# An eight-sequence, four-layer kernel: the first layer's scan moved beside the two 16-head attentions, its preparation beside the last layers

## The reference, cut to what matters

```
x = x + mamba(ln(x))            # L0: bidirectional selective scan, 256 channels, 16 states
x = x + experts16(ln(x))        # L0: 16 small experts, top 2 of the top groups
x = x + attn_relbias(ln(x))     # L1: 16 heads of 64, learned position bias
x = x + linear_with_lora(ln(x)) # L1
x = x + attn_rope(ln(x))        # L2: 16 heads of 8, rotary, causal
x = x + block(ln(x))            # L2: attention of 16 heads of 8 (rotary), norm, 8 experts
                                #     (512 wide, gelu), norm
x = x + memory(ln(x))           # L3: a recurrent outer-product memory
x = x + experts8(ln(x))         # L3: 8 experts (256 wide, gated)
```

```
xi, z = split(xn @ in_proj.T)
xc    = silu(causal_conv(xi))                     # for both directions
dt, Bm, Cm = split(xc @ xproj)
delta = softplus(dt @ dtproj + bias)
h_t   = exp(delta_t * A) * h_(t-1) + delta_t * xc_t * Bm_t   # for 16 states
y_t   = sum over states of h_t * Cm_t
out   = (0.5 * y_f + 0.5 * reversed(y_b)) * silu(z) @ out_proj.T + residual
```

## Time and profile before

| | us |
|---|---|
| median of the runs | 5811.86 |
| the profiled execution | 5812.37 |
| its span, first to last instruction | 5810.6 |
| start of sequence 0's moe0 | 225.57 |
| start of sequence 1's moe0 | 940.55 |
| start of the eighth's moe0 (z stages) | 5234.68 |

### The profile page before, as it was taken

One profiled execution on the slowest core, in us unless ns is written; L12 is line 12 of the kernel. 1 busy time (PEld: TensorE's weight loads), 2 busy tenths in 40 slices (PEclk: granted clock), 3 DMA queues, 4 the chain that ended last, 5 costly groups with the idle time before them and its releaser, 6 DMA issues. The chain is left out here.

```text
span 5810.6 us, 67170 instructions
## 1 busy us (share of the span) xinstructions
PE 4485.7 (77%) x20516; PEld 2226.2 (38%) x20516; DVE 3772.0 (65%) x8877; ACT 3064.0 (53%) x5351; POOL 1140.3 (20%) x1356
## 2 busy tenths in 40 slices
PE   5786778877788777887778777788778877788777
PEld 2342434424344243442434324343243433444334
DVE  6756586565865658656686556865668555686554
ACT  3365645556455555555655556555565555555443
POOL 2401132011320123201231012310123111231100
PEclk8996989978898788987889878897789987899778
DMA  4210021100210002100121001210012100121000
GB/s 160 87 36 1 21 65 55 32 1 25 67 55 26 1 28 71 52 22 1 34 73 47 20 1 37 75 48 13 1 42 75 46 11 1 44 73 47 7 1 2
DMA packets 104076, 218.53 MB, mean 38 GB/s; under 512 B 11072, under 2 KB 19776, under 8 KB 103152
## 3 DMA queue, kind: packets, MB, share of 16 engines
q1 hardware_dynamic: 103680, 213.81, 11.6%
HBM read 211.08 MB, written 2.69 MB: 37 GB/s over the span
## 5 line engine op out<-in xcount | busy, mean ns | idle before, releaser
L859 POOL TENSOR_TENSOR slot_work<-slot_work,slot_c_all 128x512 f32<-128x512 f32 x448 | 570.2, 1273 | 1015.9 <-DVE slot_work L942 1015.0
L777 PE MATMUL BANKS<-slot_work,WF 128*128 128x512 f32 x896 | 530.5, 679 | 5.7 <-DVE slot_du L918 2.9
L524 ACT ACTIVATE attn_prob<-BANKS 128x512 f32<-128x512 f32 (+3 forms) x896 | 401.5, 532 | 122.5 <-PE BANKS L426 119.0
L1000 PEld LDWEIGHTS BANKS<-WF,slot_x_a 128*128 128x128 f32 x2688 | 359.3, 197 | 264.5 <-ACT slot_x_a L1040 133.5
L1000 PE MATMUL BANKS<-WF,slot_x_a 128*128 128x128 f32 x2688 | 373.3, 283 | 86.3 <-ACT slot_x_a L1040 86.3
L1010 PE MATMUL BANKS<-XT,WF 128*128 128x512 f32 x768 | 425.3, 639 | 2.6 <-ACT slot_comb_t L306 2.6
L769 PE MATMUL BANKS<-slot_bcs,WB 96*128 96x512 bf16 x448 | 189.1, 422 | 305.1 <-DVE slot_work L942 304.0
L202 POOL TENSOR_TENSOR rstd<-rstd,WF 128x4 f32<-128x4 f32 x40 | 40.3, 1007 | 1572.7 <-DVE rstd L220 1559.5
L1809 DVE CUSTOM_DVE_ANT_0 attn_biased<-BANKS,attn_toep 128x512 f32<-128x512 f32 x448 | 306.0, 684 | 51.9 <-PE BANKS L1707 46.6
L1788 ACT COPY attn_probt<-BANKS 128x512 f32<-128x512 f32 x448 | 261.0, 583 | 147.3 <-PE BANKS L1714 144.4
L426 PE MATMUL BANKS<-attn_parts_kT,attn_parts_qT 64*128 64x512 bf16 (+3 forms) x896 | 309.2, 437 | 33.6 <-ACT attn_parts_qT L504 20.7
(11 more groups left out here) (674 smaller groups left out, 9464.7 us busy)
## 6 DMA issues: line engine op xcount, KB each, us to landing
slot_c_all<-c_rows SPq DMA_DIRECT2D x448, 256.0 KB, 3.1
attn_toep<-bias_line SPq DMA_DIRECT2D x112, 448.0 KB, 4.4
first_c_all<-c_rows SPq DMA_DIRECT2D x64, 256.0 KB, 3.1
WF<-in_wf SPq DMA_DIRECT2D x4, 1964.0 KB, 16.2
zattn_toep<-bias_line SPq DMA_DIRECT2D x16, 448.0 KB, 4.3
WF<-in_wf SPq DMA_DIRECT2D x3, 800.0 KB, 17.2
WF<-in_wf SPq DMA_DIRECT2D x3, 785.5 KB, 6.0
XIN<-in_x SPq DMA_DIRECT2D x8, 256.0 KB, 2.9
```

The costliest lines, as they stand in the source:

```text
L524: nc.scalar.activation(prob[:, i % PR, lo:hi], bank("T", i), ACT.Exp).then_inc(exped, 1)
L777: nc.tensor.matmul(SUM, ident, work[:, m % RW, :], start=(n == 0), stop=(n == NS - 1)).then_inc(acc, 1)
L859: nc.gpsimd.tensor_tensor(work[:, m % RW, :], work[:, m % RW, :], c_all[:, m % RC, :], ALU.mult).then_inc(rd, 1)
L1000: last = nc.tensor.matmul(DOWN[e % 2][:, j * D:(j + 1) * D], a1[:, i % 3, j * P:(j + 1) * P], w_down[:, i * D:(i + 1) * D], start=(t == 0 ...
```

## The change

The first layer becomes two functions. `mamba_pre` is its preparation and leaves its results in buffers that are kept (`M_KEPT`). `mamba_scan` is the 64 steps and the projection behind them. Its result goes to a new buffer XM, since X is still in use, and DVE copies XM to X in the last stage.

The two attentions are rewritten as streams with due times (`rope_parts`, `head8_parts`, `back_parts`; one unit is due every 1.0) and run in one block, heads, beside `mamba_scan` of the next sequence (a step is due every 3.6). `last_layers` runs in the stage last beside `mamba_pre` of the sequence after the next. Ahead of the loop there are now p0 (preparation of sequence 0), s0 (its scan, alone) and p1 (preparation of sequence 1, alone). The loop has six turns. A copy (y) does the seventh sequence: it has a scan beside its heads and no preparation. The copy z does the eighth, with neither.

The heads get four banks for everything instead of six for scores plus two for the rest, because the scan keeps three: two for its products instead of three, and one for the sum. In a step DVE now multiplies for step s and later scans the same step s. The decay ring has 4 places instead of 5, the work ring 6 instead of 8.

The weights of moe2 no longer lie in SBUF. They come by DMA, 512 KB for each expert, into a ring of three. The next input comes by DMA at the start of last, where before it came during attn1.

```diff
-    def mamba(st, after=None):
-        RD, RW, RC, AHEAD, FLUSH = 5, 8, 3, 5, 4
-        PRE, SCAN, STEP = 13.5, 52.0, 2.6
+    def mamba_pre(st, fetch):
+        PRE = 13.5
+        zs, xc, delta, du, bcs = M_KEPT
...
         def sync(sp):
+            yield -3.0
+            sp.dma_start(XIN[:, :, :], fetch()).then_inc(xin_ld, 16)
...
+    def mamba_scan(st, dest, START, STEP):
+        RD, RW, RC, LATE = 4, 6, 3, 2
+        SUM, DRIVE, OUT = PS[0], (PS[1], PS[2]), PS[1]
...
+            for s in range(STEPS):
+                d, t, n = step(s)
+                yield at(s)
+                dve.wait_ge(b_cast, s + 1)
+                V.tensor_tensor(DRIVE[s % 2], DRIVE[s % 2], du[:, d, t, :], ALU.mult).then_inc(drv, 1)
+                if s >= NS and n == LATE:
+                    yield at(s) + 0.2 * STEP
                     flush(s // NS - 1)
+                yield at(s) + 0.5 * STEP
+                dve.wait_ge(drv, s + 1)
+                dve.wait_ge(dec, s + 1)
+                if s >= RW:
+                    dve.wait_ge(acc, s - RW + 1)
+                V.tensor_tensor_scan(work[:, s % RW, :], decay[s % RD], DRIVE[s % 2], 0.0,
+                                     ALU.mult, ALU.add).then_inc(scn, 1)
...
+        def sync(sp):
+            for e in range(E if stream is not None else 0):
+                yield at - 10.0 if e < RW else at + 0.2 + step * tiles_per * (e - RW + 1)
+                if e >= RW:
+                    sp.wait_ge(used, tiles_per * (e - RW + 1))
+                sp.dma_start(ring_w[:, e % RW, :], stream[e]).then_inc(w_ld[e % RW], 16)
...
+            if copy_next:
+                dve.wait_ge(freed, 1)
+                nc.vector.tensor_copy(X[:, :, :], XM[:, :, :])
...
+    def both_attentions(st, at, u):
+        RING, WEIGH = PS[3:7], PS[7]
...
+    with Stage("p0") as st:
+        layer = mamba_pre(st, lambda: one(xs, 0))
+    with Stage("s0") as st:
+        layer = mamba_scan(st, X, 2.0, 1.95)
+    with Stage("p1", last=True) as st:
+        layer = mamba_pre(st, lambda: one(xs, 1))
...
+        with Stage("heads", last=True) as st:
+            streams = [mamba_scan(st, XM, 4.0, 3.6)] if scan_next else []
+            streams.append(both_attentions(st, 0.0, 1.0))
...
+        with Stage("last", last=True, at_end=store) as st:
+            streams = [mamba_pre(st, lambda: one(xs, b + 2))] if pre_next else []
+            streams.append(last_layers(st, scan_next))
...
+    with nc.Fori(0, n - 2) as b:
+        layers(b, True, True)
```

More of the change, by code:

```diff
@@ new lines, in back_parts, with tensor, scalar, gpsimd @@
+    def back_parts(st, tag, heads, O, turned_o, w_o, add_to, banks, at, bias=None):
+        tn, ev, dn, ch, added = (st.sem(f"{tag}_{n}") for n in ("tn", "ev", "dn", "ch", "added"))
+        def tensor(pe):
+            yield at
+            pe.wait_ge(heads.o_normed, heads.groups)
+            for j in range(NJ):
+                last = nc.tensor.transpose(banks[0][:, j * P:(j + 1) * P], O[:, j, :], ident)
+            last.then_inc(tn, 1)
+            yield at + 1.6
+            pe.wait_ge(ev, 1)
+            for j in range(NJ):
+                last = nc.tensor.matmul(banks[1][:, j * P:(j + 1) * P], turned_o[:, j * P:(j + 1) * P], w_o,
+                                        start=True, stop=True)
+            last.then_inc(dn, 1)
+        def scalar(act):
+            yield at + 0.9
+            act.wait_ge(tn, 1)
+            nc.scalar.copy(turned_o[:, :], banks[0][:, :]).then_inc(ev, 1)
+        def gpsimd(pool):
+            return
+            yield
+        def vector(dve):
+            link = Chain(dve, ch)
+            if bias is not None:
+                yield at
+                link(nc.vector.tensor_tensor(add_to[:, :, :], add_to[:, :, :], bc(bias.unsqueeze(1), [P, NJ, D]), ALU.add))
+            yield at + 2.8
+            dve.wait_ge(dn, 1)
+            nc.vector.tensor_tensor(add_to[:, :, :], add_to[:, :, :], banks[1].rearrange(tiles, j=NJ), ALU.add).then_inc(added, 1)
+        pieces = Pieces()
+        pieces.tensor, pieces.scalar, pieces.gpsimd, pieces.vector, pieces.added = tensor, scalar, gpsimd, vector, added
+        return pieces
@@ L2016, in store @@
             sp.dma_start(one(ys, b), XO[:, :, :]).then_inc(x_free, 16)
-        def clear(sp):
-            for stage in stale:
-                for s in stage.sems:
-                    sp.sem_clear(s)
-        with Stage("slot", last=True, at_end=store) as st:
-            taken = st.sem("x_taken")
-            streams = [mamba(st, after=(taken, 1))] if ahead else []
-            streams.append(last_layers(st, taken))
+        with Stage("heads", last=True) as st:
+            streams = [mamba_scan(st, XM, 4.0, 3.6)] if scan_next else []
+            streams.append(both_attentions(st, 0.0, 1.0))
```

929 lines of the change are left out of this document (481 added, 448 removed).

## The result

The changed kernel takes 5850.65 us (median of 4 runs, 5847.08 to 5863.06) against 5811.82 for the kernel before beside it: a ratio of 1.0071, 95% interval 1.0054 to 1.0089. It is slower by 0.7%, where 0.9% faster was forecast. The profiled execution has a span of 5852.3 us, 41.7 more than before.

The account below looks back on a forecast made before the run. No engine was taken as full; DVE's scan moves from slot to the attentions. Six turns of 703.2 us against 715.6 give -74, with -48, +4 and +67 elsewhere: -51, so 5760 us, range 5665 to 5885.

Parts of the forecast that it names:

- term 1: Heads with a scan, seven times: DVE's 231.9 us of work at a share of 0.843 gives 275 us.
- the share of 0.843: DVE's busy part of heads, taken from nearby rows where other layers ran beside scan steps (84% and 85%).
- Rival A: Heads set by PE and its banks, in each attention's first 25 us at clock 0.50: 290 us, 5865 total; chance 0.23.
- A's sign: Clock of 0.50 through the heads' start, and maxima or scan's multiplication waiting for PE over 40 us in a stage.
- Rival B: Heads and last together keep DVE's share of 0.68, so a turn gains nothing: 5835 us; chance 0.10.
- The argument against it: Against no gain in DVE's share: 59% alone became 84% with the scan beside; moe3 53% alone, 85% with steps.
- Rivals C and D: C: DVE at 0.91, heads 255 us, 5620 total, chance 0.15. D: last 10 us longer, 5820 total, chance 0.08.
- Terms 2 and 3: 2: last with a preparation, six times, 218.6 us. 3: seams, 6.9 us between turns, 2 between heads and last.
- Term 4: The seventh sequence (y), scan beside heads but no preparation: 667.3 us, a change of -48.
- Term 5: The eighth sequence (z), neither scan nor preparation: 187.5 us for the attentions, 2 for the seam, 2 for the rest: +4.
- Term 6: Ahead of the loop, p0, s0 and p1 in series: 238.6 us, +67, with s0 at 1.93 us a step.

Follow-up runs that it names:

- noscan: The changed kernel with no scan beside the heads in any turn (first layer's result left out): 5252.1 us.
- masked: The changed kernel with the causal maxima's masked scores written to SBUF in bf16 in place of back into their bank: 5818.4 us, ratio 1.001.
- blank: The changed kernel with the five memsets of heads due 8 later, behind GpSimd's first product: 5851.5 us, ratio 1.0088.
- port: The changed kernel with GpSimd's product with row C cut to 16 of 512 columns: 5766.2 us, ratio 0.993.
- early: The changed kernel with the matmul that spreads row B (L683) due 2.9 ahead of its multiplication in heads in place of 1.0: 5774.1 us, ratio 0.9939.
- best08: The changed kernel with L683 due 2.9 ahead, masked scores to SBUF, heads' memsets later and last's preparation due 4.5 later: 5741.7 us, ratio 0.9879.
- ring4_before: The kernel before with four banks for the scores in place of six in both attentions: 5933.3 us, ratio 1.0211.
- sum128: The changed kernel with 56 of a scan's 64 sums on TensorE cut to 128 of 512 columns: 5914.9 us, ratio 1.0181.

## Why the prediction was wrong

**The failed step** is in term 1, and it is DVE's work: 231.9 us forecast, 239.9 measured on average. The scan's part was right (239.9 less noscan's 117.3 is 122.6, with 122.1 forecast). The attentions' own 109.8 became 117.3: 3.7 us in reading the accumulators (9.0 against 5.3), 2.8 in the norm beside the memsets, some 1 in maxima that write to a bank. The change said that the attentions are rewritten as streams, and I priced them with the rows of before, instruction by instruction. At the share of 0.843 these 8 us are 9.5 of the 11.8 by which heads missed, 66 us in seven turns. The other 2.3 are the share, which was 0.836. This is arithmetic; of the runs that took added work away, masked gave 32 us and blank was inconclusive.

**The reason given for the share** failed too: that the order of instructions supports it, as "DVE mostly finds its input ready". In the measured heads DVE waited for PE most of all at L738, 20.8 us in turn 2, and moving one matmul of 0.42 us by 1.9 due units took 77 us from the kernel. The rows of the order shown ahead of the prediction had L683 behind a sum and two scores. A sum of busy times doesn't see this, nor does a share taken from slot: there the scan had three banks and one more step between its multiplication and its scan. That the share came so near all the same is luck. Port shows that 9.4 us of DVE's time are waits for GpSimd, part of which may have stood in slot's 122.1 already, and early, with 238.9 us of DVE's work in 276.2, shows that 0.865 was to be had.

**Rival A** gave 5865, nearest to the result, and some of it was seen: turns with a clock of 0.84 (291.9 us) stand beside turns with 0.87 (280.9). Had all seven lasted 280.9, the kernel would have been some 41 us shorter, by this estimate about the time of the kernel before. But A's place was wrong. In the first 25 us from each attention's first score the clock was 0.86 and 0.85 in turn 2, not 0.50:

```profile
1244.80:1269.80 25.00, 22.35 (x109) 8.35 (x108) 22.96 (x67) 14.52 (x25) 8.47 (x9) 0.86 0.24 71
1377.60:1402.60 25.00, 21.71 (x99) 7.61 (x98) 23.43 (x37) 12.18 (x21) 7.51 (x6) 0.85 0.17 53
```

The maxima and the multiplication waited 28 us for PE in turn 2 and 38 in turn 4, under the 40 that A's sign asked for. Why the clock fell in some turns and not in others, with the same instructions, and whether it made them longer or followed from it, stays open. **Rival B** (5835) was 16 us off, where A was 14. Its share of 0.68 didn't stay, but over heads and last of turn 2 together it rose only to 0.71 (358.7 us of DVE's work in 507.8), with more work, and a turn gained 2.4 us on average (19 in best08). B leant on the Trainium skill (Perfetto Trace Analysis, Optimization Strategy). That section says that interleaving may help where the most-contended engine changes over time. It doesn't say that nothing is gained elsewhere, and the rows don't show its condition missing: PE is the busiest in both attentions (62.1 and 70.0 us, with DVE at 48.3 and 61.5), and DVE in the scan alone (115.1, with PE at 88.5). The argument against it misread a row as well: in moe3 alone PE was busiest, 42.3 of 45.3 us. **Rivals C and D** didn't come: heads had 0.84 and not 0.91, and last took 215 to 218 us to its last DVE instruction, as forecast.

**Terms 2 and 3** held nearly: 229.1 us from DVE's last busy instruction in heads to the next moe0, with 227.5 forecast. DVE began last 5.9 us behind that instruction, with 2 and 3.3 forecast. In turn 2 no engine waited for the weights that are streamed. **Term 4** missed by 16 (683.5 us from y's moe0 to z's, 667.3 forecast), all of it in heads (293.4). **Term 5** missed by 12: it had no price for the new form of the attentions but 2 us for the rest. Noscan shows the same 203 us in every turn, and ring4_before that fewer banks alone can cost 15. **Term 6** was 6 us low. Most steps of s0 took 1.85 us, less than the 1.93 forecast, but ten of 63 took 2.1 to 3.8, so that the mean was 1.97, and XIN came 3.2 us after DVE was free.

## What to carry to other kernels

When two streams share in-order engines, look at each short instruction that another engine waits for, and ask what stands ahead of it and since when its buffer has been free; put it as early as the buffer allows. Moving one matmul of 0.4 us that way was worth 77 us here, nearly as much as taking away almost all of GpSimd's product. When code is rewritten on the way to being moved, price it anew: where it writes, and what now runs beside it. And look at every turn of a loop, not at one: the same text took 281 us in one turn and 293 in another.

## What the hardware showed

- Taking some 47 us of matmul columns (an estimate, 0.84 us from each of 56 sums) from a stage of 281 us made it slower: the granted clock fell from 0.87 to 0.68, and the stage took 294.5 us. The Trainium skill (TensorE: Matmul & The Clock Gate, What's actually happening) says that the gate follows how busy the array has lately been. The trace agrees in that the clock fell when work was taken away; PE's busy share of the whole stage doesn't show it, 0.77 (216.3 of 280.9) in the changed kernel and 0.76 (225.3 of 294.5) in sum128.
- Reading the accumulator after a causal maximum took 142 ns when its elements went to PSUM (noscan, port) and 83 ns when they went to SBUF, whether in fp32 (the kernel before) or in bf16 (masked).
- Two of the norm's four instructions took 2.38 us together while GpSimd ran a memset; all four take 1.11 without one:

```profile
1210.18 1.32 POOL L1174 MEMSET heads_vals<- 128x1472 f32 x1
...
1210.26 2.38 DVE L424 TENSOR_SCALAR XN<-X,mv,rstd 128x128 f32<-128x128 f32 x2 [1.12 <-POOL rstd L396]
```
